# Reordering both ends of a batched attention block: group 3's x, Wq's low parts, one bias part, and the tail's low products

## The reference

```python
xn = layernorm(x, g_in)
q = (xn @ Wq) * DH ** -0.5              # 16 heads of 64
k, v = split(xn @ Wkv)                  # one key/value head; a null key and value are put first
sim = q @ k.T + bias                    # bias [16, 128, 128], null column in front
sim = where(causal & mask, sim, -max)
out = softmax(sim) @ v
return x + layernorm(out @ Wo, g_out)
```

## Time and profile before

| | |
|---|---|
| median of the timed runs | 1037.13 us (3 runs, 1036.7 to 1037.44) |
| the profiled execution's own time | 1034.55 us |
| its span, first to last instruction | 1032.4 us |
| mean granted TensorE clock | 0.995 of full speed |
| TensorE busy | 1001.6 us, 97% |
| weight loads | 879.1 us, 85% |
| GpSimd busy | 832.7 us, 81% |
| VectorE busy | 767.8 us, 74% |
| ScalarE busy | 661.4 us, 64% |

### The profile page before, as it was taken

The page is one execution under the profiler, slowest core; times in us unless marked ns, Lnnn a source line. Parts: engine busy times, 40 slices in busy tenths (PEclk is TensorE's granted clock), DMA queues, the critical chain, the costliest instruction groups (busy, mean ns, idle before and its releaser), DMA issues.

```text
span 1032.4 us, 43753 instructions
## 1 busy us (share of the span) xinstructions
PE 1001.6 (97%) x14250; PEld 879.1 (85%) x14250; DVE 767.8 (74%) x3549; ACT 661.4 (64%) x2621; POOL 832.7 (81%) x1507
## 2 busy tenths in 40 slices
PE   6898999999999999999999999999999999999986
PEld 5787888888888888888888888888888889888874
DVE  5867787777787777787777787777787777876664
ACT  6755675666676665676665676665676575676562
POOL 5767888888888888888888888888888888888775
PEclk9998999999999999999999999999999999999999
DMA  8422323223233232323223232332323323222112
GB/s 238 135 62 69 84 68 88 75 65 101 66 93 83 77 89 55 106 69 86 77 70 97 64 104 72 79 86 55 108 67 87 85 65 98 61 68 67 44 32 62
DMA packets 93774, 84.04 MB, mean 81 GB/s; under 512 B 25328, under 2 KB 67824, under 8 KB 93552
## 3 DMA queue, kind: packets, MB, share of 16 engines
q1 hardware_dynamic: 92496, 81.05, 29.7%
q10 hardware_dynamic: 1056, 0.04, 0.1%
HBM read 40.12 MB, written 16.78 MB: 55 GB/s over the span
## 4 chain that ended last, share of the span: by engine, by line
PE 88%; POOL 2%; issue 1%; DVE 1%; ACT 1%; POOLq 0%; DVEq 0%; ACTq 0%
PE ps_proj L548 39%; PE ps_pv L536 32%; PE ps_s L497 10%; PE ps_pv L522 8%; POOL y_out L1226 0%; POOL y_nrm L1222 0%; POOL w_nrm L1182 0%; POOL bias_b L1173 0%; ACT exp_bot L985 0%; ACT exp_top L985 0%; POOL small L1208 0%; DVE logit_bot L670 0%; ACT o_hi L994 0%; DVE wt L686 0%; DVE logit_top L670 0%
## 5 line engine op out<-in xcount | busy, mean ns | idle before, releaser
L985 ACT ACTIVATE exp_bot<-logit_bot,neg_max 128x129 f32<-128x129 f32 x512 | 201.8, 398 | 225.9 <-DVE neg_max L670 220.5
L1173 POOL TENSOR_TENSOR bias_b<-bias_c,mask_add 128x256 f32<-128x256 f32 (+1 forms) x512 | 296.2, 608 | 31.9 <-DVE neg_max L670 31.7
L548 PE MATMUL ps_proj<-xt_hi,wq_hi 128*128 128x256 f32 x1024 | 302.4, 295 | 9.3 <-DVE q_sb L754 6.2
L548 PE MATMUL ps_proj<-xt_hi,wq_lo 128*128 128x256 f32 x1024 | 288.4, 282 | 0.0
L548 PE MATMUL ps_proj<-xt_lo,wq_hi 128*128 128x256 f32 x1024 | 288.3, 281 | 0.0
L670 DVE CUSTOM_DVE_ANT_0 logit_bot<-ps_s,bias_b 128x128 f32<-128x128 f32 x512 | 129.5, 289 | 161.9 <-PE ps_s L497 139.9
L548 PEld LDWEIGHTS ps_proj<-xt_hi,wq_hi 128*128 128x128 f32 x1024 | 193.6, 189 | 24.9 <-issue 11.5
L1182 POOL TENSOR_TENSOR w_nrm<-exp_bot,w_inv 128x256 f32<-128x256 f32 x256 | 157.2, 614 | 70.0 <-DVE w_inv L679 66.5
L548 PEld LDWEIGHTS ps_proj<-xt_hi,wq_lo 128*128 128x128 f32 x1024 | 194.1, 190 | 0.7 <-issue 0.6
L536 PE MATMUL ps_pv<-wo_hi,o_hi 128*128 128x512 f32 x488 | 193.1, 396 | 1.3 <-ACT o_hi L994 1.3
L548 PEld LDWEIGHTS ps_proj<-xt_lo,wq_hi 128*128 128x128 f32 x1024 | 193.8, 189 | 0.0
(11 more groups left out here) (110 smaller groups left out, 1743.7 us busy)
## 6 DMA issues: line engine op xcount, KB each, us to landing
x_in<-in_x_dram SPq DMA_DIRECT2D x32, 512.0 KB, 4.0
x_split<-xn SPq DMA_DIRECT2D x480, 32.0 KB
v_rep<-v_raw SPq DMA_DIRECT2D x256, 32.0 KB
x_res<-in_x_dram SPq DMA_DIRECT2D x128, 64.0 KB, 1.9
x_res<-in_x_dram SPq DMA_DIRECT2D x64, 128.0 KB, 2.5
out_dram<-y_out SPq DMA_DIRECT2D x128, 64.0 KB, 1.7
out_dram<-y_out SPq DMA_DIRECT2D x64, 128.0 KB, 2.3
w_raw<-in_L_cond_Wq_dram SPq DMA_DIRECT2D x4, 512.0 KB, 7.1
```

The source lines that it names most:

```text
L548: mm = pe.matmul(ps[:, 0:TOK], w[:, k, cols], xt[:, slot, k], start=(j == 0), stop=(j == len(todo) - 1))
L985: ins = nc.scalar.activation(out_[:, s, j], in_[:, s, j], ACT.Exp, bias=neg_max[:, s, k:k + 1], scale=-1.0, accum_out=w_sum[:, s, k:k + 1])
L1173: ins = nc.gpsimd.tensor_tensor(out_, bias, key_mask, ALU.add)
```

## The change

Nothing that is computed changes; five things are done in another order or place.

- **Head, group 3's x.** Its statistics and aggregation (VectorE) move from the end of `first_group` to right behind `heads_lo` of batch 0; its rstd moves ahead of bias 8 and `normalize` 7 on GpSimd, its `x_norm` ahead of `x_high` of group 2 on ScalarE. VectorE's `mask_of(1, 1)` moves from before the first q copy of group 1 to behind these. SP's `load_mask` that waits for it moves behind `split_x(2)`.
- **Head, Wq.** The high and low parts 1 come ahead of the key/value copies (ScalarE) and of mask and q copy 0 (VectorE). Low part 3 comes between logits 0 and logits 1. ScalarE takes q copy 3.
- **Head, bias.** The last bias part (c = 3) is made by VectorE: for each of two heads one tensor_scalar and two scalar_tensor_tensor over 64 columns, which subtract the null bias and add the causal mask at once. GpSimd makes three parts.
- **Head, others.** Biases, q copies, `wo` parts, transposes and inverses change places; the heads of batch 0 come ahead of the exponentials of tile 7.
- **Tail.** `spread_v`, `out_stats` and `y_scale` of batch 60 come first; transposes come later and logits sooner; the heads of batch 62 come ahead of exponentials 15 and their inverse; the output projection is split in a high and a low function, and the low products of two half-batches stand behind the next values.

The diff, cut:

```diff
@@ -434,16 +435,20 @@
             def body(p, first, loads, last):
-                if not last:
+                def next_mask():
                     sp.wait_ge(mask_made, 2 * p + 2)
                     apart(sp)
                     load_mask(p + 1, 1)
+
+                if not (first or last):
+                    next_mask()
                 if loads:
                     sp.wait_ge(xn_made, GB * (2 * p + 3))
                     apart(sp)
                     load_x(p + 2, 0)
                 if first:
                     split_x(BY_PE)
+                    next_mask()
                 else:
                     store(p, -2, True)
                 spread_v(2 * p + 1)
...
@@ -525,18 +530,27 @@
                             if r == len(ITEMS[g % 2]) - 1:
                                 mm.then_inc(pv_done, 1)
-            def project_out_half(batch, u):
-                hi, lo = heads_of(batch)
-                todo = [(hi, w, c) for c in range(CB) for w in (wo_hi, wo_lo)] + [(lo, wo_hi, c) for c in range(CB)]
+            def project_out_high(batch, u):
+                hi, _ = heads_of(batch)
                 wait(pe, o_hi_made, 4 * batch + 2 + 2 * u)
                 wait(pe, o_lo_made, 4 * batch + 1 + 2 * u)
-                for j, (o, w, c) in enumerate(todo):
-                    if j == 2 * CB:
-                        wait(pe, o_lo_made, 4 * batch + 2 + 2 * u)
-                    mm = pe.matmul(out_bank(batch)[:], o[:, u, c], w[:, 2 * c + u], start=(u == 0 and j == 0),
-                                   stop=(u == 1 and j == len(todo) - 1))
+                for c in range(CB):
+                    for w in (wo_hi, wo_lo):
+                        pe.matmul(out_bank(batch)[:], hi[:, u, c], w[:, 2 * c + u],
+                                  start=(u == 0 and c == 0 and w is wo_hi), stop=False)
+
+            def project_out_low(batch, u):
+                _, lo = heads_of(batch)
+                wait(pe, o_lo_made, 4 * batch + 2 + 2 * u)
+                for c in range(CB):
+                    mm = pe.matmul(out_bank(batch)[:], lo[:, u, c], wo_hi[:, 2 * c + u], start=False,
+                                   stop=(u == 1 and c == CB - 1))
                 if u == 1:
                     mm.then_inc(o_done, 1)
+
+            def project_out_half(batch, u):
+                project_out_high(batch, u)
...
@@ -645,11 +659,13 @@
                 pe.wait_ge(q_made, QT * GROUPS)
                 project_out_half(B_LAST - 1, 0)
                 scores(p, CG + 6)
-                project_out_half(B_LAST - 1, 1)
+                project_out_high(B_LAST - 1, 1)
                 values(p, B_LAST, 2)
+                project_out_low(B_LAST - 1, 1)
                 project_out_half(B_LAST, 0)
+                project_out_high(B_LAST, 1)
                 values(p, B_LAST + 1, 3)
-                project_out_half(B_LAST, 1)
+                project_out_low(B_LAST, 1)
                 pe.wait_ge(s_read, 2 * CP * PAIRS)
                 project_out(B_LAST + 1)
...
@@ -786,6 +802,29 @@
                 nc.vector.tensor_tensor(wo_piece(wo_lo, i), raw_piece(i, OT // WP), wo_piece(wo_hi, i).bitcast(F32),
                                         ALU.subtract).then_inc(wo_lo_made, 1)
+            def bias_of_last():
+
+                c = CB - 1
+                dve.wait_ge(ld_bias, 16 * BIAS_LOADS)
+                dve.wait_ge(nb_made, 2)
+                dve.wait_ge(causal_made, 2)
+                dve.wait_ge(early_filled, 6)
+                raw_late, raw_early = bot_top(bias_raw[:, c])
+                late, early = bot_top(bias_c[:, c])
+                for e in range(2):
+                    null = nb_row[:, c, e:e + 1]
+                    nc.vector.tensor_scalar(
+                        late[:, e, 0:HALF].rearrange("p (a j) -> p a j", j=BLK),
+                        early_swapped(raw_late[:, :, 0:HALF])[:, e], null, None,
+                        ALU.subtract).then_inc(last_bias_made, 1)
+                    nc.vector.scalar_tensor_tensor(
+                        out=late[:, e, HALF:N], in0=raw_late[:, e, HALF:N], scalar=null, in1=causal[:],
+                        op0=ALU.subtract, op1=ALU.add).then_inc(last_bias_made, 1)
+                    nc.vector.scalar_tensor_tensor(
+                        out=early[:, e].rearrange("p (a j) -> p a j", j=BLK), in0=early_swapped(raw_early)[:, e],
+                        scalar=null, in1=causal_early[:].rearrange("p (a j) -> p a j", j=BLK),
+                        op0=ALU.subtract, op1=ALU.add).then_inc(last_bias_made, 1)
+
             def first_group():
                 def q_copies(f, *tiles):
                     for i in tiles:
...
@@ -801,21 +840,21 @@
                 x_low_of(0, True)
                 wq_low(0)
+                wq_low(1)
                 mask_of(0, 0)
                 q_copies(0, 0)
-                wq_low(1)
                 x_stats_of(0, 1)
                 x_mean_var_of(1)
-                q_copies(0, 1)
+                q_copies(0, 1, 2)
                 wq_low(2)
-                q_copies(0, 2, 3)
                 logits(0, 0)
+                wq_low(3)
                 logits(1, 1)
-                wq_low(3)
                 inverse(0, 0)
-                inverse(1, 1)
                 x_stats_of(1, 0)
                 x_mean_var_of(2)
+                bias_of_last()
+                inverse(1, 1)
                 x_low_of(1, True)
                 wo_low(0)
                 logits(2, 2)
...
@@ -823,35 +862,36 @@
                 turn(0)
                 wo_low(1)
                 inverse(2, 2)
-                mask_of(1, 1)
-                dve.wait_ge(bias_made, 3 * CB)
+                dve.wait_ge(bias_made, 3 * (CB - 1))
+                dve.wait_ge(last_bias_made, 6)
                 q_copies(1, 0)
+                logits(4, 4)
                 inverse(3, 3)
-                logits(4, 4)
                 logits(5, 5)
+                spread_v_of(0, 0)
                 q_copies(1, 1)
                 turn(2)
+                q_copies(1, 2)
+                inverse(4, 4)
+                logits(6, 6)
+                inverse(5, 5)
+                logits(7, 7)
                 wo_low(2)
-                inverse(4, 4)
-                q_copies(1, 2)
-                inverse(5, 5)
-                spread_v_of(0, 0)
-                logits(6, 6)
-                logits(7, 7)
                 q_copies(1, 3)
                 wo_low(3)
                 q_copies(1, 4)
                 inverse(6, 6)
-                turn(4)
                 for g in range(4):
                     heads_lo(0, g)
+                x_stats_of(1, 1)
+                x_mean_var_of(3)
+                turn(4)
+                mask_of(1, 1)
                 q_copies(1, 5)
                 inverse(7, 7)
                 turned(BY_PE)
                 mask_of(2, 0)
                 x_low_of(BY_PE, False)
-                x_stats_of(1, 1)
-                x_mean_var_of(3)
             def body(p, first, loads, last):
                 if first:
...
@@ -918,11 +958,12 @@
                     for g in range(4):
                         heads_lo(batch, g)
+                spread_v_of(F_LAST, 1)
+                out_stats(B_LAST - 2, 0)
+                out_mean_var(B_LAST - 2, 0)
                 logits(N_LAST, CG)
-                out_stats(B_LAST - 2, 0)
+                logits(N_LAST + 1, CG + 1)
                 front(F_LAST, 1, "q", 6)
-                out_mean_var(B_LAST - 2, 0)
-                logits(N_LAST + 1, CG + 1)
                 front(F_LAST, 1, "q", 7)
                 turn(-2)
                 inverse(N_LAST, CG)
@@ -930,23 +971,22 @@
                 inverse(N_LAST + 1, CG + 1)
                 logits(N_LAST + 3, CG + 3)
                 heads(B_LAST - 1)
-                turn(0)
                 inverse(N_LAST + 2, CG + 2)
-                spread_v_of(F_LAST, 1)
                 logits(N_LAST + 4, CG + 4)
                 inverse(N_LAST + 3, CG + 3)
                 logits(N_LAST + 5, CG + 5)
+                turn(0)
+                logits(N_LAST + 6, CG + 6)
+                inverse(N_LAST + 4, CG + 4)
                 turn(2)
-                inverse(N_LAST + 4, CG + 4)
-                logits(N_LAST + 6, CG + 6)
                 inverse(N_LAST + 5, CG + 5)
                 logits(N_LAST + 7, CG + 7)
                 turn(4)
                 inverse(N_LAST + 6, CG + 6)
-                inverse(N_LAST + 7, CG + 7)
+                heads(B_LAST)
                 out_stats(B_LAST - 1, 1)
                 out_mean_var(B_LAST - 1, 1)
-                heads(B_LAST)
+                inverse(N_LAST + 7, CG + 7)
                 turn(6)
                 heads(B_LAST + 1)
                 out_stats(B_LAST, 2)
...
@@ -1081,11 +1121,12 @@
                 x_high_of(0, True)
                 wq_high(0)
+                wq_high(1)
                 act.wait_ge(shifts_made, 2)
                 front(0, 0, "kv", 0)
-                wq_high(1)
                 wq_high(2)
```

(21 more changed lines are left out.)

11 lines of the change are left out of this document (7 added, 4 removed).

## The result

| | before | after |
|---|---|---|
| timed, median | 1036.91 (1035.77 to 1037.44, 4 executions) | 1030.5 (1029.87 to 1033.17, 4) |
| ratio | | 0.9941, interval 0.9925 to 0.9956 |
| profiled execution, its span | 1034.55, 1032.4 | 1033.17, 1031.4 |

The two profiled executions lie only 1.4 apart: that of before is 2.4 under its median, that of after 2.7 above its own.

The account below looks back on a forecast made before the run. TensorE, busy 97% of the span, bounds the kernel, so only time before 88 us or after 991 us counts. Profiled 1034.55 - 3.7 (head) + 0.3 (tail) = 1031.15; with 2.58 to the median, 1033.7; range 1031.0 to 1036.0.

Parts of the forecast that it names:

- First scores 1.6 sooner: Step 1, head: reordered Wq parts and ScalarE's q tile 3 start the scores of 24.09 at about 22.5.
- Six bias instructions, 1.3 us: Step 2, head: VectorE's last bias part costs 1.3 us; scores of 42.78 start about 40.8, inverse 3 and logits 5 1.9 sooner.
- `o_lo` end 49.45: Step 3, head: without bias waits and with transposes behind it, VectorE's o_lo ends 4.2 us sooner; first output product moves along.
- xn end at 55.7: Step 4, head: group 3's x statistics start at 49.5, so ScalarE's xn ends at 55.7 instead of 62.3.
- Mask at 52.8 and split at 59.3: Step 5, head: SP's mask load waits for VectorE's mask and gates group 3's split, which starts 3.7 us sooner.
- Restart at 78.15: Step 6, head: TensorE restarts at about 78.15 instead of 81.85, reaching its stall at 74.35, idle 3.8 us instead of 4.70.
- I leave the 2.3 us of slow clock in place: Step 6, head: the 2.3 us lost to slow clock behind TensorE's restart stay, since no row says they shorten.
- rival C: Head: idle before the restart shrinks enough to keep the clock up, 2.3 us more gained: 1031.4; chance 0.12.
- The 2.58 that the forecast carried over: Sum: before's timed median, 1037.13, lies 2.58 above its profiled execution; the same difference was added to the forecast.
- The tail: forecast +0.3: Tail: handovers of GpSimd, ScalarE and VectorE end 0.3 us later, bounds -0.6 to +1.5; values at 1008.5, last projection 1020.2 to 1020.7.
- Rival D: Tail: the 2.4 us idle before the values grows and the clock falls there, at most 2.3 us: 1036.0; chance 0.07.
- Rivals B and E: SP's mask wait, head: B takes back most of the gain, 1035.9, chance 0.15; E turns it to loss, 1039.4, chance 0.05.

Follow-up runs that it names:

- after_again: The changed kernel run once more with no edit, giving its second trace; 1029.24 us, ratio 0.9936 to before.
- head_only: The kernel before with only the change's edits up to the loop, the tail as before; 1029.66 us, ratio 0.9939.
- pool_bias: The changed kernel with the last bias part made by GpSimd again instead of VectorE; 1031.63 us, ratio 0.9938 to before.
- late execution: First profiled execution of the changed kernel, its first xn 0.8 later than in the trace of before; timed median 1030.5 us, ratio 0.9941.
- mask_load_later: The changed kernel with SP's first next-mask load behind the eight v_rep issues of group 1; 1029.67 us, ratio 0.9925 to before.
- tail_only: The kernel before with only the change's tail edits; 1035.84 us, ratio 0.9995.
- before_filled: The kernel before with 15 unread products of 128 columns in TensorE's idle time ahead of 81.9 us; 1072.51 us, ratio 1.0331.
- before_fill3: The kernel before with 3 unread products of 512 columns in TensorE's idle time ahead of 81.9 us; 1045.01 us, ratio 1.0077.
- early_products: The kernel before with 3 unread products of 128 columns behind the warming ones at the start, idle time unfilled; 1044.56 us, ratio 1.0089.
- fill3_warm2: The kernel before with 3 unread products of 512 columns ahead of 81.9 us and 2 warming products instead of 5; 1038.22 us, ratio 1.0025.
- x_early_only: The kernel before with only group 3's x statistics, rstd and xn moved early; 1029.57 us, ratio 0.9931.
- both_better: The changed kernel with the edits of mask_load_later and turn_early together; 1027.19 us, ratio 0.9905 to before.
- late_x: The changed kernel with group 3's statistics, rstd and xn back at the ends of the lists; 1034.83 us, ratio 0.9976 to before.
- turn_early: The changed kernel with the transposes of tiles 8 and 9 ahead of tile 13's logits in the tail; 1029.55 us, ratio 0.9926 to before.
- before_again: The kernel before run once more with no edit, for a second trace; 1036.56 us, ratio 0.9997.
- x_new_tail: The kernel before with the edit of x_early_only and the tail of turn_early; 1029.03 us, ratio 0.9938.

## Why the prediction was wrong in size

Point by point, by its own steps:

1. First scores 1.6 sooner: 1.1 to 1.2 (22.95 in the second trace, 22.85 in head_only, against 24.09).
2. Six bias instructions, 1.3 us: they took 1.5, from 30.39 to 31.9. The scores of 42.78 came at 42.50, and at 41.67 in the second trace, without the late start: 1.1 sooner, not 1.9. And VectorE's bias part is not what won it: pool_bias has them at 41.24 without it.
3. `o_lo` end 49.45: 50.74 in the late execution, 49.9 without its delay.
4. xn end at 55.7: 56.9, or 56.1.
5. Mask at 52.8 and split at 59.3: 53.9 and 60.81; in the second trace 53.1 (the load at 53.20) and 59.98, 3.0 sooner instead of 3.7. The two halves of the mask took 0.80 us, near the 0.9 allowed and not 0.3 above it. The gate is confirmed by mask_load_later.
6. Restart at 78.15: 78.25 and 77.73. The place was right, but in part by luck: the split came 1.5 and 0.7 later than forecast, and the landing made up for it. From the end of the 16 issues to VectorE's transpose it took 2.59 us in the trace of before (74.20 to 76.79), and I carried that over; in both traces of the changed kernel it took 1.28. The traces show what differs. Over these 2.6 us before has one transfer of the kind "instruction", 16 KB, from 74.64 to 75.70; the changed kernel has none over its 1.28:

```profile
q1 hardware_dynamic: 307, 0.14, 21.6%
q8 instruction: 1, 0.02, 2.6%
```

```profile
q1 hardware_dynamic: 162, 0.07, 21.4%
```

(the first from 74.2 to 76.8 in before, the second from 71.38 to 72.66 in the second trace; packets, MB, share). So it is in all 17 traces: where such a transfer began within 0.9 us of the end of the issues it took 2.5 to 2.9 (both of before, tail_only, before_filled, before_fill3, early_products), in each of the others 1.27 or 1.28. No run moves that transfer alone, so this is a coincidence seen in every trace, not a cause shown.

**Here the step failed: "I leave the 2.3 us of slow clock in place".** It rested on an idle time of 3.8 us, and that was mis-sized. I let TensorE reach the stall 2.8 sooner; it reached it 0.9 sooner (78.25 - 2.03 = 76.22, against 77.15), since the wait of 61.19 took back two of the three microseconds won up to the output product. The 1.4 that I allowed for it named the right cause (a q copy behind `xt_lo`, behind xn on ScalarE) at too small a price, and the output product itself came 3.0 sooner, not 4.2 (0.8 of this is the late start). So the idle time was 2.0 to 2.4 us, and at about that size the clock held in the second trace and in those of head_only (1.8) and pool_bias (2.3), and fell in part in the first.

This is rival C, given 0.12: 1031.4, against 1030.5 measured. What the runs show for it: after idle times of 4.5 to 5.0 us ahead of the restart (both traces of before, tail_only, early_products) the 24 products took 4.6 to 5.25 each time; with idle times under 1.8 or none (before_filled, fill3_warm2, head_only, x_early_only, both_better, mask_load_later) they always ran at full clock there; between 2.0 and 2.8 it went either way (4.58 and 4.43 after 2.03 and 2.12, 3.10 after 2.3, 2.37 and 2.8). In late_x and turn_early the granted clock was 0.83 from 60 to 70 us instead, behind the wait of 61 us (2.10 and 1.78). Shorter stalls cost clock elsewhere too: in the loop of before_filled seven of the ten of 1.4 to 2.0 us did. And rival C's own sign, 2.83 us ahead of 1012.95 without loss, was luck of that trace: the same wait cost clock in before_again (2.83) and head_only (2.85). The timed executions agree on the whole: the mean granted clock was 0.9943 over 67 of before, 0.9967 over 10 of the changed kernel, 0.998 over those of x_early_only and of both_better. The difference of 0.0024, of 1030 us, is 2.5 us of work lost: an estimate, near the 2.3 that the forecast left in place (2.15 by the rows, since 24 products at full clock take 3.10 and not 2.97). With a restart 4.1 sooner that makes 6.3 to 6.6, less the tail. The 2.58 that the forecast carried over from before's first trace to its median did not carry over: the medians of the changed kernel lie 2.7 below its first trace and 1.1 below its second.

The tail: forecast +0.3, measured +0.75 in the traces at full clock, and in the rows all as said but 0.1 to 0.5 late. On the clock of before (1.75 later than the rows shown) values 1008.85 (1008.5 forecast), product 1011.96 (1011.5), last projection 1020.77 (1020.2 to 1020.7). GpSimd's `normalize` of tile 10 did wait for the transposes, 2.91 us:

```profile
1002.31 0.61 POOL L1224 TENSOR_TENSOR w_nrm<-exp_bot,w_inv 128x256 f32<-128x256 f32 x1 [2.91 <-DVE wt L702]
```

Rival D's fall of the clock in the tail is real, but old: it was there in traces of both tails (before_again 0.83 from 1010 to 1020, head_only 0.75 and after_again 0.83 from 1000 to 1010), and none of it in x_early_only, both_better and x_new_tail. With the changed kernel's tail and its 2.33 us of idle time it fell in four of six traces, with the 0.7 of turn_early in none of three. It is a part of why before's median stands above its first trace, from which the forecast was made. Rivals B and E, SP's gate, are out: the load came at 53.1 to 54.0.

What stays open: why the loop takes 908.76 to 911.41 us over these traces, with small stalls that have no releaser, and whether the change has a part in that; what decides about the clock at idle times of 1.4 to 3 us; and what holds up the landing in the traces of before.

## What to carry to other kernels

When a stall is shortened, work out its idle time on both sides, the restart and the arrival; where the idle time was long enough to cost clock, the clock's price is a term of its own that can fall away as a whole. Here one moved chain (statistics, rstd, xn) gives the whole gain by itself; the other edits of the head give 2.5 us without it (late_x) and none that shows on top of it, since they only bring TensorE sooner to the same landing. The two tests show it together: gains behind one wait do not add. And one trace has a luck of its own: two kernels with medians 6.4 apart had first traces 1.4 apart.

## What was not expected of the hardware

Three more products ahead of the loop (six matmul instructions by the page, 14256 against 14250, and as many weight loads), in TensorE's idle time and with nothing else changed, cost 9 us (1044.56, ratio 1.0089, early_products): 14 stalls of up to 1.2 us at projection products inside the loop, for which the view of waits names no releaser; with fifteen (14280) it was 35 us, 13 such stalls of up to 2.0 and the slow clock behind seven of them. With three taken out again elsewhere (fill3_warm2, 14250) 0.5 us of them were left. A pair of them in early_products, 62.7 us apart; a pass of TensorE's loop (eight rows of scores) takes 61.6 without a stall, and the loop has 14 passes, so there is one stall in each:

```profile
229.59 0.28 PE L548 MATMUL ps_proj<-xt_hi,wq_hi 128*128 128x256 f32 x1 [0.64 <-issue]
...
292.33 0.28 PE L548 MATMUL ps_proj<-xt_hi,wq_hi 128*128 128x256 f32 x1 [1.18 <-issue]
```

The runs show that the count ahead of the loop decides. The Trainium skill, "Runtime: NRT & Kernel Launch", section "Instruction fetch mechanics", says that a taken branch whose target lies outside the instructions held near the engine forces a fetch before it can go on, and that blocks of instructions are fetched in order; a loop whose place against these blocks is moved would stall once a pass, as here. The traces hold such transfers. The view of the DMA queues from 225 to 232 us in early_products, around the first of the two rows, has

```profile
q8 instruction: 2, 0.03, 2.1%
```

of 16 KB each, and the first of them lasts from 227.37 to 228.34; TensorE goes on at 229.59. In early_products all 14 stalls end 1.2 to 1.6 us after the end of a 16 KB transfer of this kind, and so do the 13 at projection products in before_fill3 and all 17 in before_filled. Before has a transfer at the like place, from 225.7 to 227.1, and no stall there. So most likely TensorE waits there for its own instructions: this is read from the times of the two, since the trace names no releaser, and whether the branch or a mere boundary of blocks brings the fetch no run here shows.
